# Attention: the last two maxima pieces of each pair of steps moved between the products of the two steps before

## The reference

```python
q = _rope(q)
k = _rope(k)
scores = jnp.einsum('bhqd,bhkd->bhqk', q, k) / np.sqrt(D)
causal = jnp.tril(jnp.ones((t, t), dtype=bool))
scores = jnp.where(causal, scores, -jnp.inf)
attn = jax.nn.softmax(scores, axis=-1)
out = jnp.einsum('bhqk,bhkd->bqhd', attn, v).reshape(b, t, c)
return out @ out_w.T + out_b
```

## Time and profile before

| | us |
|---|---|
| median of 3 runs | 1494.61 (1493.98 to 1494.83) |
| profiled execution | 1494.09 |
| its span on the core | 1492.4 |
| attention, first score matmul to last products | about 303 |
| TensorE busy / VectorE busy / ScalarE busy, whole span | 1444.6 / 925.8 / 609.3 |

### The profile page before, as it was taken

One profiled execution on the slowest core, in us unless ns is written; L12 is line 12 of the kernel. 1 busy time (PEld: TensorE's weight loads), 2 busy tenths in 40 slices (PEclk: granted clock), 3 DMA queues, 4 the chain that ended last, 5 costly groups with the idle time before them and its releaser, 6 DMA issues. The chain is left out here.

```text
span 1492.4 us, 22392 instructions
## 1 busy us (share of the span) xinstructions
PE 1444.6 (97%) x7696; PEld 1074.0 (72%) x7696; DVE 925.8 (62%) x1841; ACT 609.3 (41%) x1007; POOL 544.0 (36%) x455
## 2 busy tenths in 40 slices
PE   7999999999999999999999999999999999999887
PEld 5788777788888888888888785555555557777554
DVE  6887887855544553555243476666666467667654
ACT  5343455622431341243121114555555736343544
POOL 0333243302430441143052223444444576104773
PEclk9999999999999999999999998999999999999999
DMA  6111446503320421131445887877774464844336
GB/s 212 42 57 57 173 162 240 198 29 104 113 94 0 157 96 56 43 126 56 178 145 176 250 239 209 216 193 192 199 195 143 167 237 161 325 159 142 102 102 241
DMA packets 105228, 223.38 MB, mean 150 GB/s; under 512 B 9329, under 2 KB 35313, under 8 KB 104241
## 3 DMA queue, kind: packets, MB, share of 16 engines
q1 hardware_dynamic: 101392, 211.96, 43.9%
q0 software_dynamic: 3744, 10.23, 2.2%
HBM read 157.54 MB, written 64.36 MB: 149 GB/s over the span
## 5 line engine op out<-in xcount | busy, mean ns | idle before, releaser
L968 POOL TENSOR_TENSOR ff_w_lo<-ff_raw,ff_w_hi 128x1024 fp32r<-128x1024 f32 x64 | 153.8, 2404 | 219.9 <-ACT ff_w_hi L998 205.8
L115 PE MATMUL op_bank<-ff_x_hi,ff_w_lo 128*128 128x512 f32 x512 | 199.3, 389 | 0.2 <-issue 0.2
L117 PE MATMUL op_bank<-ff_x_hi,ff_w_hi 128*128 128x512 f32 x512 | 199.3, 389 | 0.0
L116 PE MATMUL op_bank<-ff_x_lo,ff_w_hi 128*128 128x512 f32 x512 | 199.2, 389 | 0.0
L1238 DVE TENSOR_TENSOR ff_h_lo<-ff_hf,ff_h_hi 128x512 f32 (+1 forms) x64 | 143.4, 2241 | 54.6 <-ACT ff_h_hi L1126 54.3
L2090 ACT ACTIVATE at_pt<-at_st 128x512 f32<-128x512 f32 (+1 forms) x286 | 144.8, 582 | 69.9 <-PE at_st L2133 68.5
L1386 DVE CUSTOM_DVE_ANT_0 mx_mx<-mx_mx,mx_mask 128x128 f32<-128x128 f32 (+2 forms) x202 | 102.3, 515 | 35.8 <-PE mx_mx L1374 34.6
L998 ACT ACTIVATE ff_w_hi<-ff_raw 128x1024 fp32r<-128x1024 f32 x64 | 67.8, 1061 | 114.3 <-PE op_bank L117 111.2
L115 PEld LDWEIGHTS op_bank<-ff_x_hi,ff_w_lo 128*128 128x128 f32 x512 | 96.1, 188 | 20.5 <-issue 0.6
L117 PEld LDWEIGHTS op_bank<-ff_x_hi,ff_w_hi 128*128 128x128 f32 x512 | 96.1, 188 | 20.2
L116 PEld LDWEIGHTS op_bank<-ff_x_lo,ff_w_hi 128*128 128x128 f32 x512 | 96.1, 188 | 20.2
(11 more groups left out here) (478 smaller groups left out, 3431.4 us busy)
## 6 DMA issues: line engine op xcount, KB each, us to landing
ff_raw<-in_Wug SPq DMA_DIRECT2D x64, 512.0 KB, 3.6
at_raw<-in_expert_gu SPq DMA_DIRECT2D x16, 704.0 KB, 7.9
mx_qp<-q_hi SPq DMA_DIRECT2D x12, 512.0 KB, 6.4
mx_kp<-k_hi SPq DMA_DIRECT2D x12, 512.0 KB, 10.6
at_raw<-in_expert_d SPq DMA_DIRECT2D x8, 768.0 KB, 9.6
expert_gu_bf<-at_cast SPq DMA_DIRECT2D x16, 352.0 KB, 5.7
ex_e_gu<-expert_gu_bf SPq DMA_DIRECT2D x8, 704.0 KB, 8.2
tm_ln_res<-in_x SPq DMA_DIRECT2D x4, 1024.0 KB, 5.3
```

The source lines that it names most:

```text
L115: pe.matmul(out, cut_l(ll), cut_r(rh), start=first, stop=False, **kw)
L116: pe.matmul(out, cut_l(lh), cut_r(rl), start=False, stop=False, **kw)
L117: return pe.matmul(out, cut_l(lh), cut_r(rh), start=False, stop=last, **kw)
L968: pool.tensor_tensor(w[j][1][:, :, :, :], raw[:, j], f32(w[j][0][:, :, :, :]), ALU.subtract)\
```

## The change

The last two pieces of every pair (`BETWEEN = 2`) are taken out of the second step's scores. They are issued in the same run's product part, after the products of the first step and ahead of those of the second. In the very first run, which has no products, they follow the scores. No instruction is added or taken away, and the other engines' lists are as before; only TensorE's order changes.

```diff
+    BETWEEN = 2
...
+        def woven(u, s):
+
+            return pieces_at(u, s)[:-BETWEEN] if s % PAIR == PAIR - 1 else pieces_at(u, s)
...
-                pieces = pieces_at(u, s)
+                pieces = woven(u, s)
...
                 if before:
-                    for s in before[1]:
+                    for s, mine in zip(before[1], steps):
                         pv(before[0], s)
+                        if mine == steps[0]:
+                            for of, n in pieces_at(u, steps[-1])[-BETWEEN:]:
+                                mx.piece(pe, of, of % SLOTS, of // SLOTS, n)
+                else:
+                    for of, n in pieces_at(u, steps[-1])[-BETWEEN:]:
+                        mx.piece(pe, of, of % SLOTS, of // SLOTS, n)
                 if TURN_STEP in steps and u + 1 < UNITS:
                     mx.turn(pe, u + 1)
```

## The result

The changed kernel takes 1498.74 us in the median of 11 runs (1496.79 to 1503.70), the kernel before 1494.96 (1493.81 to 1497.34). The ratio is 1.0031, 95% interval 1.0023 to 1.0040: 4.6 us slower, 3.4 to 6.0; the medians are 3.8 apart. A second comparison gave 1.0022 (1.0012 to 1.0033). I had forecast 1500.1, 0.37% slower.

The account below looks back on a forecast made before the run. TensorE was taken as the path throughout, held up by VectorE and ScalarE in the score parts; borders 14.8, pieces 15.1 and turn 3.4 less 27.5 saved gave +5.8 us on 1494.09, forecast 1500.1, range 1495.5 to 1504.0.

Parts of the forecast that it names:

- The border, 0.37: TensorE's switch out of and into products costs 0.37 us for each place, 40 places, 14.8 us.
- The score parts: The six score parts of a unit shorten with two pieces fewer, 27.5 us saved in all.
- The limits: What ends each shortened score part: an exponential in (0,1), (2,3), (4,5), (10,11); reductions in (6,7); ScalarE late in (8,9).
- The turn: After the last pair's late pieces TensorE waits 0.47 us for the join before each of seven turns, 3.4 us.
- The first run: It has no products; its late pieces only change places with scores, keeping its length to a few tenths.
- The sum: 14.8 + 15.1 + 3.4 - 27.5 = +5.8 us, giving a forecast of 1500.1 us, 0.37% slower.
- Pieces: Late pieces leave the score parts and are paid beside the products, 15.1 us in all.
- The cheap border: Rival: a border inside a product part costs 0.10, so 40 insertions cost 4.0 us and time is 1489.5; chance 0.07.
- "No change": Rival: the turn doesn't wait and score parts shorten some tenths more, within 3 us of before; chance 0.13.
- "Dearer": Rival: waits only move, exponentials hold the scores in (6,7), less is saved, 1507 or 1503.5; chance 0.15.
- The waits: TensorE's 20.7 us of waits for reductions would be mostly gone and the wait for exponentials grown.

Follow-up runs that it names:

- the half-way kernel: Against the kernel before: late pieces only in the run of (8,9), between the two halves of the first step's products; 1.0011, 1.6 us slower.
- the held-back scores: Kernel before, with one or two score matmuls of the last unit's runs held back between the two steps' products; 1494.56 us in one run.
- the kernel with (6,7) and (10,11): Late pieces between products only in the runs of these two pairs, against the kernel before; 0.9974, 3.9 us faster.
- the even deal with a place: Pieces dealt (4, 3, 4, 4, 4, 4, 4, 3, 4, 4), last two between products in (4,5) only, against the kernel before; 0.9985, 2.2 us faster.
- the even deal: Kernel before, no piece between products, pieces dealt to steps as (4, 3, 4, 4, 4, 4, 4, 3, 4, 4); 0.9988 (0.9970 to 1.0005), median 1491.48.

## Why the prediction was right

- **The border, 0.37.** Right: 0.35 to 0.38 in five of the changed kernel's six places in a unit and 0.41 in that of (4,5), and 0.33 to 0.40 by itself in the last unit. It was read from the two borders that every product part already had. The drain that the Trainium skill's TensorEngine Tiling (Array Packing), section Tiling Modes, gives for a changed tiling mode is there at the new borders too (0.13 us more on the products and 0.22 around the pieces). The Trainium skill's TensorE: Matmul & The Clock Gate, section Architectural detail, says that TensorE's queue can pull weight loads ahead; had it done so here, the second late piece would follow the 256-wide one by about 0.12, as a 256-wide piece is followed in the score part (1002.00 to 1002.12). It follows by 0.23 (1006.27 to 1006.50).
- **The score parts.** Forecast 2.60, 2.60, 2.61, 2.80, 3.94 and 3.77; measured 2.55, 2.54, 2.60, 2.75, 3.87 and 3.73. Each was forecast 0.01 to 0.07 too long, 0.28 a unit; over the kernel they give back 29.4 us instead of the 27.5 of the sum. This is the mis-sized term. Where in the chain of releases the difference was lost I did not test. The limits were right for the four that end on an exponential and for (8,9), where hardly anything came back. For (6,7) the limit was wrong: I had its last pieces held by the second and third reductions, and the trace shows waits for exponentials only. That 2.80 came so near to 2.75 was partly luck.
- **The turn.** Forecast 0.47, measured 0.50, and the half-way kernel removed exactly this. (Seven times 0.47 is 3.3, where the sum has 3.4.)
- **The first run.** I gave it nothing, and no change can be read there. It and the run of (2,3) behind it took 12.35 us together before (905.56 to 917.91) and take 12.48 now (904.93 to 917.41), 12.76 in the second trace of the changed kernel. The clock is at its lower level in most of this stretch and rises at another point in each execution.
- **The sum.** +5.8 forecast, +3.7 in the traces and 3.3 to 4.6 by the times; a unit of about 39.6 forecast, 39.35 measured. Pieces, borders and turn were forecast at 2.27 + 2.22 + 0.47 = 4.96 us a unit, and they cost 0.55 + 4.41 = 4.96. So the error lies in the score parts: 0.28 a unit, 1.9 us in all. Most of the other 0.2 is in the first two runs, where the sum had +0.28 and the traces have +0.13.
- **The rivals.** The cheap border is refuted by the held-back scores. "No change" needed a turn without a wait, and it waits. "Dearer" was right that exponentials would hold the scores of (6,7), and wrong in the price: no part gave back less than forecast.
- **The waits.** I said that the 20.7 us for reductions would be mostly gone. The view still lists 13 us under that name; most of it is the loader's idle time beside the products, and only (8,9) keeps a real one.

## What to carry to other kernels

Interleaving two kinds of matmul that use the array in different shapes has a price, here 0.33 to 0.41 us for a change of shape and the change back, that can be read from any border already in the trace; count the borders before moving work between them. Balance each stretch by itself: the change was one good place (-0.60 us a unit) and one bad one (+0.86), two that cost 0.32 together and two that came out even. A place can pay only by the waits it takes away, so look for the part that waits longest, whichever helper it waits for. Where a helper engine is overloaded only in some stretches, try first to deal its work out evenly, which by the traces gave 3.3 us here with no border, though the times leave it unclear; and ask of every piece that is moved later who waits for the last of them.

## What the runs showed of the hardware that I had not expected

Executions of one kernel differ by several us here, with the same instructions. The granted clock of the profiled executions shows one reason. All of them have a half-clock stretch at the start of the attention, of 10 us (13.7 in the kernel with (6,7) and (10,11)). Most have besides one or two of 3.4 us elsewhere, such as that from 849.7 us on in the kernel with (6,7) and (10,11) (start:end, length, busy us of the five engines, clock, DMA share, GB/s):

```profile
849.20:852.60 3.40, 2.70 (x7) 2.25 (x8) 1.03 (x5) 0.63 (x1) 1.35 (x2) 0.58 0.58 221
845.80:849.20 3.40, 2.20 (x9) 1.18 (x7) 3.40 (x6) 1.84 (x4) 1.35 (x2) 1.00 0.94 294
```

The clock is 0.58 of the full 2.4 GHz in the first stretch, mostly at the lower level of 1.2, after a stretch at 1.00 in which TensorE was busy for 2.20 of 3.40 us. What such a stretch costs can be read where it falls into a dense part: the run of (10,11) of the seventh unit takes 8.44 us in the half-way kernel and 8.41 in the even deal with a place, which have such a stretch there, and 6.76 in the kernel before, so 1.7 us. The kernel before and both executions of the changed one had none between the attention's start and the last ten microseconds, nor ahead of it.

The recorded mean clocks tell how much of the spread this is. Over the 192 executions that have one, each compared with others of its kernel, the time falls by about 1.0 us for each 0.001 of granted clock, with a correlation of -0.71: about half of the variance goes with the clock, and what makes the other half stays open. These differences are why I judged the experiments by a unit's period beside the ratios. The period repeats within 0.1 us in an execution, but for the last period of the two kernels with the even deal.
